# Expert stage of a cross-attention and mixture-of-experts kernel: groups kept in flight over more steps, with sixteen row buffers in place of eight

## Chip, cores and metric

The kernel runs on one core of one Trainium2 chip. The metric is the device time of one execution in microseconds (us), lower is better; several executions are timed and their median is given. Profiles are of one execution.

## What is computed

Input x is (32, 256, 256): 32 sequences of 256 tokens with 256 features; ctx has the same shape. Cut to what matters:

```python
x = x + xattn(layernorm(x), ctx, Wq1, Wk1, Wv1, Wq2, Wk2, Wv2, alpha, Wout, bout)
# and then the part that the change is in, over the 32*256 = 8192 tokens:
h = layernorm(x)
probs = softmax(h @ gate_w.T)                 # 16 experts
w, idx = top_k(probs, 4); w = w / sum(w)      # each token goes to 4 experts
g, u = h @ w1[e], h @ w3[e]                   # 256 -> 128, for expert e
out = sum over the 4 experts of w * ((silu(g) * u) @ w2[e])    # 128 -> 256
x = x + out
```

## The kernel before

**Stages.** The program has three stages, one after the other. The attention stage works through the 32 sequences in one loop; it also computes the router, sorts each normalised token into the region of each of its four experts in a DRAM table `x_rows` (a scatter by GpSimd, line 504), and counts. A short plan (lines 953 to 970) then makes a table of 144 groups: 8192*4/256 = 128 full groups of 256 rows and room for 16 more, since each expert's last group is padded. Each group belongs to one expert. The last stage (lines 461 to 469 and 1003 to 1019) reads four result rows for each token, weights them and adds.

**The expert stage** is what the change is about. All five engines run the same loop over groups, written by `stage_b` (line 355): the groups up to number `LOADS` are written out, then a hardware loop runs over passes of `LOADS` groups each, then the last ones are written out again. `LOADS` is 8, so TensorE's loop has 16 passes. `group(j, r)` holds what an engine does in step j (r = j mod `LOADS`), and the calls `if exists(j - 1)` say on which group each operation works. Matrix products are made from split operands: a number is kept as a rounded `hi` part and a rest `lo`, and three passes (hi*hi, hi*lo, lo*hi, `PASSES`) make one product.

In step j the engines do, in this order:

- SyncE (`load_group`, lines 442 to 455): reads the row number of group j from `table_row`, and starts the load of its 256 rows from `x_rows` into row buffer `xg[r]`. For j of 8 and above it first waits until TensorE has transposed group j - 8 (`xg_t`) and until the results of group j - 8 have been scattered (`y_sent`), since the scatter takes its row indices from the row buffer.
- TensorE (`group`, line 1280): transposes the rows of group j + 1 (`p_xt`, line 1289, 4 matmuls); reads the expert number of group j into a register (`expert_of`, line 1276) and makes gate and up of group j (`p_gu`, line 1300, 12 matmuls); transposes the gated values of group j - 1 (`p_at`, line 1310, 2 matmuls); makes the down projection of group j - 2 (`p_y`, line 1318, 6 matmuls). In the first two steps of a pass it also reads the expert of group j - 2 again, since registers don't outlive the pass (line 1281).
- ScalarE (line 691): tanh of group j - 1 into `gated` (696), `actT_hi` of group j - 2 (701), `y_out` of group j - 3 (706, waits for the scatter that used the same of four buffers), `xgT_hi` of group j + 1 (711).
- VectorE (line 978): the two products of the gating for group j - 1 (983, 986), `actT_lo` of j - 2 (992), `xgT_lo` of j + 1 (998).
- GpSimd (`return_group`, line 539): when `y_out` of group j is set, two indirect DMAs (line 544) scatter its 256 rows into `y_rows`.

Every PSUM result of this stage (`p_xt`, `p_gu`, `p_at`, `p_y`) has two buffers, taken in turn. The waits that a step rests on are the `wait` lines beside each operation, such as TensorE's before gate and up:

```python
pe.wait_ge(xgT_lo, j + 1)      # the split rows of group j
wait(pe, act_set, j - 1)       # p_gu's buffer, read by the gating of group j - 2
```

**Memory.** The weights' `lo` parts for the experts are made late from twelve 4 KB pieces a partition (`late_slots`, line 162) that are loaded a second time after the attention stage has released their space; the row buffers, `wgu_lo` and `wdn_lo` lie behind them.

Of the kernel before, what the change touches and what calls it, by code (L numbers as in the profile page):

```python
# [6 lines left out]
F32 = mybir.dt.float32  # L7
# [38 lines left out]
def xattn_moe_kernel(nc, x, ctx, Wq1, Wk1, Wv1, Wq2, Wk2, Wv2, alpha_attn, Wout, bout,  # L46
# [22 lines left out]
    MOST = TOKENS // GROUP  # L69
    DUMP = TOKENS * TOP_K  # L70
    PIECE = KT * INNER
    LOADS = 8
    TC = -(-GROUPS // P)
    assert S == 2 * P and D == 2 * P and INNER == 4 * P and I == P and B >= 4 and B % 4 == 0
    assert math.frexp(SCALE)[0] == 0.5
# [8 lines left out]
    with ExitStack() as stack:  # L84
        def sb(name, shape, dt=F32, stack=stack):
            return stack.enter_context(nc.sbuf_tensor(name, shape, dt))
# [72 lines left out]
            slotf = small("slotf", [P, ST, TOP_K])  # L159
            slot_i = small("slot_i", [P, ST, TOP_K], I32)  # L160
        with ExitStack() as later:
            late_slots = [sb(f"late_slot{i}", [P, PIECE], stack=later)[:, :] for i in range(E // 2 + E // 4)]
            wgu_lo = sb("wgu_lo", [P, E, KT, 2, I], F32R, later)
            wdn_lo = sb("wdn_lo", [P, E, D], F32R, later)
            wgu = [wgu_hi, wgu_lo]
            wdn = [wdn_hi, wdn_lo]
# [6 lines left out]
            y_out = [sb(f"y_out{i}", [P, 2, D], stack=later) for i in range(4)]  # L173

            plan = lambda name, shape, dt=F32: sb(name, shape, dt, later)
# [189 lines left out]
        def exists(j):  # L365

            return not isinstance(j, int) or 0 <= j < GROUPS
# [16 lines left out]
        def _(sp):  # L384
# [72 lines left out]

# [94 lines left out]
        def _(act):  # L552
# [136 lines left out]
            pad_experts(act, range(1, E, 2))  # L689

            def group(j, r):
                if exists(j - 1):
                    i = (r + 1) % 2
                    act.wait_ge(gu_done, j)
                    wait(act, act_t, j - 2)
                    act.activation(gated[i][:, :, :], p_gu[:, i, :, 0:I], ACT.Tanh, scale=0.5).then_inc(tanh_done, 1)
                if exists(j - 2):
                    i = r % 2
                    act.wait_ge(act_t, j - 1)
                    wait(act, down_done, j - 3)  # L700
                    act.copy(flat(actT[i][0][:, :, :]), p_at[:, i, 0:2 * P]).then_inc(actT_hi, 1)
                if exists(j - 3):
                    i, o = (r + 1) % 2, (r + 1) % 4
                    act.wait_ge(down_done, j - 2)
                    wait(act, y_sent[o], 8 * (j - 3 - o))
                    act.copy(flat(y_out[o][:, :, :]), flat(p_y[:, i, :, :])).then_inc(y_set, 1)
                if exists(j + 1):
                    i = (r + 1) % 2
                    act.wait_ge(xg_t, j + 2)
                    wait(act, gu_done, j)  # L710
                    act.copy(flat(xgT[i][0][:, :, :, :]), flat(p_xt[:, i, :, :, :])).then_inc(xgT_hi, 1)  # L711

            stage_b(act, group, before=1, after=3)


            for r in range(4):
# [12 lines left out]
        def _(dve):  # L729
# [246 lines left out]
                dve.tensor_tensor(lo, slot, hi.bitcast(F32), ALU.subtract).then_inc(late_lo, 1)  # L976

            def group(j, r):
                if exists(j - 1):
                    i = (r + 1) % 2  # L980
                    dve.wait_ge(tanh_done, j)

                    dve.scalar_tensor_tensor(gated[i][:, :, :], gated[i][:, :, :], 1.0, p_gu[:, i, :, 0:I],
                                             ALU.add, ALU.mult).then_inc(gate_step, 1)
                    dve.wait_ge(gate_step, j)
                    dve.tensor_tensor(gated[i][:, :, :], p_gu[:, i, :, I:2 * I], gated[i][:, :, :],  # L986
                                      ALU.mult).then_inc(act_set, 1)
                if exists(j - 2):
                    i = r % 2
                    dve.wait_ge(actT_hi, j - 1)  # L990
                    wait(dve, down_done, j - 3)
                    dve.tensor_tensor(flat(actT[i][1][:, :, :]), p_at[:, i, 0:2 * P],
                                      flat(actT[i][0][:, :, :]).bitcast(F32), ALU.subtract).then_inc(actT_lo, 1)
                if exists(j + 1):
                    i = (r + 1) % 2
                    dve.wait_ge(xgT_hi, j + 2)
                    wait(dve, gu_done, j)
                    dve.tensor_tensor(flat(xgT[i][1][:, :, :, :]), flat(p_xt[:, i, :, :, :]),  # L998
                                      flat(xgT[i][0][:, :, :, :]).bitcast(F32), ALU.subtract).then_inc(xgT_lo, 1)
            stage_b(dve, group, before=1, after=2)  # L1000


            def total(b, r, loads):
# [19 lines left out]
        def _(pe):  # L1023
# [254 lines left out]
            experts = {}  # L1278

            def group(j, r):  # L1280
                if exists(j - 2) and r < 2:
                    experts[(r - 2) % LOADS] = expert_of(j - 2)
                if exists(j + 1):
                    i = (r + 1) % 2
                    pe.wait_ge(xg_in[(r + 1) % LOADS], xg_loads(j + 1, r + 1))
                    wait(pe, xgT_lo, j)
                    for n in range(2):
                        for k in range(KT):
                            mm = pe.transpose(p_xt[:, i, n, k, :], xg[(r + 1) % LOADS][:, n, k * P:(k + 1) * P], ident[:, :])  # L1289
                    mm.then_inc(xg_t, 1)  # L1290
                if exists(j):
                    i = r % 2
# [12 lines left out]
                if exists(j - 1):  # L1305
                    i = (r + 1) % 2
# [5 lines left out]
                if exists(j - 2):  # L1312
                    i = r % 2
                    pe.wait_ge(actT_lo, j - 1)
                    wait(pe, y_set, j - 3)
                    for n in range(2):
                        for m, (h, a) in enumerate(PASSES):
                            mm = pe.matmul(p_y[:, i, n, :], actT[i][h][:, n, :],  # L1318
                                           wdn[a][:, bass.ds(experts[(r - 2) % LOADS], 1), :].rearrange("p e d -> p (e d)"),
                                           start=(m == 0), stop=(m == 2))  # L1320
# [32 lines left out]
```

## Time and profile before

| | |
|---|---|
| median of 3 executions | 2157.95 us (2154.18 to 2159.37) |
| profiled execution | 2155.32 us, of which its span is 2153.5 us |
| attention stage and plan | 0 to about 1576 us of the span |
| expert stage, first row transpose to end of last scatter's issue | 1579.5 to 2006.8 us |
| last stage | 2008 to 2153.5 us |
| TensorE busy over the span | 1907.1 us (89%) |
| VectorE, ScalarE, GpSimd busy | 1417.3, 1261.0, 1211.3 us |

Busy time is that of an engine's own work; reading a register, a branch or a wait doesn't count. The profile names TensorE's two halves PE (matmuls) and PEld (weight loads, which overlap them); DVE is VectorE, ACT ScalarE, POOL GpSimd, SP SyncE. A name with a q behind it (PEldq, POOLq, SPq) is the engine's sequencer: register reads, branches, DMA issues. In the slices of the page TensorE is nine tenths busy or more in almost all of the attention stage and of the expert stage, and falls off between the two and in the last stage.

### The profile page before, as it was taken

To read this page: it belongs to the slowest core of one execution; us is meant where nothing else is said; L and a number is where in the kernel's file an instruction comes from. 1 tells how busy PE (TensorE), PEld (TensorE's weight loads), DVE (VectorE), ACT (ScalarE), POOL (GpSimd) and SP (SyncE) were. 2 spreads that over 40 slices of the span, in tenths; PEclk is the share of its full clock that TensorE was granted. 3 is DMA by queue.
4 is the path that set the end of the run, shared out by engine and by line. 5 is a ranking of instruction groups with operands and counts; after the bars stand their busy time and mean duration, and the time that the engine had idled before them with its cause. 6 is when DMAs were issued, how large, how long until landed. Compare 5 with 4: busy or idle time off the path is not lost.

```text
span 2153.5 us, 53309 instructions
## 1 busy us (share of the span) xinstructions
PE 1907.1 (89%) x15778; PEld 1642.3 (76%) x15779; DVE 1417.3 (66%) x3205; ACT 1261.0 (59%) x3605; POOL 1211.3 (56%) x1683
## 2 busy tenths in 40 slices
PE   5999999999999999999999999999369999999100
PEld 4788888888888878888888888878269999999100
DVE  4567666667666666766666766666536666666577
ACT  4766666676666666666666666667136556555100
POOL 2466666566666566666566666556426666666200
PEclk9999999999999999999999999999679999999655
DMA  5610111101111110111101111110766666666798
GB/s 149 153 36 35 42 49 47 34 34 34 39 49 49 34 34 34 39 45 48 39 34 34 38 45 49 39 34 26 189 158 184 180 182 179 184 184 179 276 371 317
DMA packets 158596, 210.54 MB, mean 98 GB/s; under 512 B 24273, under 2 KB 131425, under 8 KB 158562
## 3 DMA queue, kind: packets, MB, share of 16 engines
q1 hardware_dynamic: 119394, 127.75, 20.7%
q0 software_dynamic: 26112, 71.86, 9.2%
q10 hardware_dynamic: 13056, 10.50, 1.7%
q8 instruction: 18, 0.29, 0.1%
q14 instruction: 16, 0.13, 0.0%
HBM read 113.02 MB, written 97.03 MB: 98 GB/s over the span
## 4 chain that ended last, share of the span: by engine, by line
PE 82%; DMA 7%; issue 3%; DVE 3%; SPq 3%; POOL 2%; ACT 1%; DVEq 0%; POOLq 0%; ACTq 0%
PE p_s L1047 12%; PE p_av L1145 12%; PE p_pt L1129 12%; PE p_s L1111 10%; PE p_gu L1300 9%; PE p_x L1180 5%; PE p_y L1318 4%; PE p_s L1057 4%; DMA z<-mid_rows 3%; PE p_xt L1289 3%; DMA out_dram<-z 2%; PE p_x L1047 2%; PE p_pt L1047 2%; PE p_av L1057 2%; PE p_pt L1057 2%
## 5 line engine op out<-in xcount | busy, mean ns | idle before, releaser
L512 POOL TENSOR_TENSOR probs<-probs,inv 128x256 f32<-128x256 f32 x1024 | 596.0, 614 | 434.0 <-DVE inv L844 433.3
L603 ACT ACTIVATE probs<-p_s,nmx 128x256 f32<-128x256 f32 x1024 | 475.3, 488 | 67.5 <-DVE nmx L837 62.7
L837 DVE TENSOR_REDUCE nmx<-p_s 128x4 f32<-128x1024 f32 x256 | 313.1, 1223 | 140.3 <-PE p_s L1111 136.7
L544 POOL DMA_INDIRECT y_rows<-y_out,xg x288 | 276.3, 959 | 177.8 <-issue 107.9
L504 POOL DMA_INDIRECT x_rows<-routed,slot_i x256 | 252.5, 986 | 170.0 <-DVE target L829 95.8
L1129 PEld LDWEIGHTS p_pt<-ident,probs 128*128 128x128 f32 x2048 | 222.2, 141 | 87.5 <-issue 62.4
L1129 PE MATMUL p_pt<-ident,probs 128*128 128x128 f32 x2048 | 280.0, 280 | 7.5 <-issue 4.9
L1145 PE MATMUL p_av<-probsT,val 128*64 128x256 f32 x2048 | 280.0, 394 | 6.5 <-DVE probsT L741 5.8
L741 DVE COPY probsT<-p_pt 128x512 f32<-128x512 f32 x256 | 176.1, 688 | 109.8 <-PE p_pt L1129 107.1
L1047 PE MATMUL p_s<-rowsT_hi,wp_hi 128*128 128x256 f32 x768 | 231.6, 302 | 8.3 <-DVE wp_lo L857 8.3
L591 ACT COPY probsT<-p_pt 128x512 f32<-128x512 f32 x256 | 152.5, 596 | 137.4 <-PE p_pt L1129 117.3
L603 ACT ACTIVATION_READ_ACCUMULATOR probs<-p_s,nmx 128x1 f32 x1024 | 223.4, 218 | 0.0
L1047 PE MATMUL p_s<-rowsT_hi,wp_lo 128*128 128x256 f32 x768 | 218.3, 284 | 0.0
L1047 PE MATMUL p_s<-rowsT_lo,wp_hi 128*128 128x256 f32 x768 | 218.2, 284 | 0.0
L1145 PEld LDWEIGHTS p_av<-probsT,val 128*64 128x64 f32 x2048 | 130.6, 137 | 76.1 <-issue 5.2
L1300 PE MATMUL p_gu<-wgu_hi,xgT_hi 128*128 x576 | 175.1, 304 | 6.1 <-DVE gated L986 4.3
L1111 PE MATMUL p_s<-kT_hi,qT_hi 64*128 64x256 f32 x1024 | 167.2, 323 | 2.4 <-DVE qT_lo L860 2.4
L1300 PE MATMUL p_gu<-wgu_hi,xgT_lo 128*128 x576 | 163.0, 283 | 0.0
L1300 PE MATMUL p_gu<-wgu_lo,xgT_hi 128*128 x576 | 161.9, 281 | 0.0
L998 DVE TENSOR_TENSOR xgT_lo<-p_xt,xgT_hi 128x512 fp32r<-128x512 f32 x144 | 99.6, 692 | 85.0 <-ACT xgT_hi L711 85.0
L1047 PEld LDWEIGHTS p_s<-rowsT_hi,wp_hi 128*128 128x128 f32 x768 | 147.7, 192 | 8.9 <-issue 8.7
L1047 PEld LDWEIGHTS p_s<-rowsT_lo,wp_hi 128*128 128x128 f32 x768 | 148.3, 193 | 0.0
(183 smaller groups left out, 4712.5 us busy)
## 6 DMA issues: line engine op xcount, KB each, us to landing
xg<-x_rows SPq DMA_DIRECT2D x144, 257.0 KB
y_in<-y_rows SPq DMA_DIRECT2D x32, 1024.0 KB, 6.7
rows<-in_ctx_dram SPq DMA_DIRECT2D x32, 256.0 KB, 2.7
x_in<-in_x_dram SPq DMA_DIRECT2D x32, 256.0 KB, 2.7
mid_rows<-x_mid SPq DMA_DIRECT2D x32, 256.0 KB, 2.2
z<-mid_rows SPq DMA_DIRECT2D x32, 256.0 KB, 7.4
out_dram<-z ACTq DMA_DIRECT2D x32, 256.0 KB, 5.7
y_rows<-y_out,xg POOLq DMA_INDIRECT x288
```

The lines of the kernel that those rows point to most:

```text
L504: pool.indirect_dma_start(x_rows, bass.IndirectOffsetOnAxis(ap=slot_i[:, t, k:k + 1], axis=0), routed[:, t, k, :], None).then_inc(rows_sen ...
L512: pool.tensor_tensor(pr[:, h, t, :], pr[:, h, t, :], rc[:, g:g + 1].to_broadcast([P, S]), ALU.mult).then_inc(normed_p, 1)
L544: pool.indirect_dma_start(y_rows, bass.IndirectOffsetOnAxis(ap=xg[r][:, i, D:D + 1].bitcast(I32), axis=0), y_out[r % 4][:, i, :], None).th ...
L603: act.activation(probs[u % 2][:, h, t, :], p_s[:, 2 * (u % 2) + h, t * S:(t + 1) * S], ACT.Exp, bias=nmx[u % 2][:, g:g + 1], accum_out=sum ...
L741: dve.tensor_copy(flat(probsT[:, 1, :, :]), p_pt[:, 1, :]).then_inc(pt_out_b, 1)
L837: dve.tensor_reduce(nmx[i][:, :], p_s[:, 2 * i:2 * i + 2, :].rearrange("p h (t k) -> p (h t) k", t=ST), AX.X, ALU.max, negate=True).then_i ...
L1047: mm = pe.matmul(proj_bank(n)[:, j * S:(j + 1) * S], wp[a][:, w, k, c:c + P], rowsT[w // 3][r][:, k, :], start=(i == 0), stop=(i == 5))
L1057: mm = pe.matmul(proj_bank(n), rowsT[w // 3][r][:, k, t * P:(t + 1) * P], wp[a][:, w, k, :], start=(i == 0), stop=(i == 5))
L1111: mm = pe.matmul(p_s[:, 2 * d + h, t * S:(t + 1) * S], qT[d][q][r:r + HEAD_DIM, p, t * P:(t + 1) * P], kT[d][k][r:r + HEAD_DIM, p, :], sta ...
L1129: mm = pe.transpose(p_pt[:, h, k * S + t * P:k * S + (t + 1) * P], probs[u % 2][:, h, t, k * P:(k + 1) * P], ident[:, :])
L1145: mm = pe.matmul(p_av[r:r + HEAD_DIM, 0:S], val[d][:, k, c:c + HEAD_DIM], probsT[:, h, k, :], start=(d == 0 and k == 0), stop=(d == 1 and ...
L1300: mm = pe.matmul(p_gu[:, i, n, :], xgT[i][h][:, n, k, :], wgu[a][:, bass.ds(experts[r], 1), k, :, :].rearrange("p e g i -> p (e g i)"), st ...
```

## The change

What it does, engine by engine:

- `LOADS` is 16: sixteen row buffers, and a hardware loop over passes of sixteen groups (7 passes), with more steps written out before and behind it.
- TensorE's step j now works on: rows of j + 2, gate and up of j, gated values of j - 2, down projection of j - 4. It reads the expert of j - 4 again in the first four steps of a pass.
- ScalarE's step: `xgT_hi` of j + 1 first, tanh of j - 1, `actT_hi` of j - 3, `y_out` of j - 5. VectorE's: `xgT_lo` of j + 1 first, the gating of j - 1, `actT_lo` of j - 3.
- GpSimd's step is as it was, in passes of sixteen. SyncE waits for group j - 16 before it loads group j.
- Memory: the eight new row buffers and the small tiles take the place of the weight pieces, so loads from the ninth on wait until the `lo` weights are made; `wgu_lo`, `wdn_lo` and the first eight row buffers stay where they were.

```diff
-    LOADS = 8
+    LOADS = 16
...
-            late_slots = [sb(f"late_slot{i}", [P, PIECE], stack=later)[:, :] for i in range(E // 2 + E // 4)]
...
-            xg = [sb(f"xg{i}", [P, 2, ROW], stack=later) for i in range(LOADS)]
+            with ExitStack() as loading:
+                late_slots = [sb(f"late_slot{i}", [P, PIECE], stack=loading)[:, :] for i in range(E // 2 + E // 4)]
+
+            xg_more = [sb(f"xg{i}", [P, 2, ROW], stack=later) for i in range(LOADS // 2, LOADS)]
...
             for r in range(LOADS):
+                if r == LOADS // 2:
+                    sp.wait_ge(late_lo, LATE)
                 load_group(r, r)
...
-                    sp.wait_ge(y_sent[r % 4], 32 * (2 * q + r // 4 - 1))
+                    sp.wait_ge(y_sent[r % 4], 32 * (LOADS // 4 * (q - 1) + r // 4 + 1))
...
# ScalarE, group(j, r)
+                if exists(j + 1):
+                    i = (r + 1) % 2
+                    act.wait_ge(xg_t, j + 2)
+                    wait(act, gu_done, j)
+                    act.copy(flat(xgT[i][0][:, :, :, :]), flat(p_xt[:, i, :, :, :])).then_inc(xgT_hi, 1)
                 if exists(j - 1):
...
-                if exists(j - 2):
-                    i = r % 2
-                    act.wait_ge(act_t, j - 1)
-                    wait(act, down_done, j - 3)
+                if exists(j - 3):
+                    i = (r + 1) % 2
+                    act.wait_ge(act_t, j - 2)
+                    wait(act, down_done, j - 4)
                     act.copy(flat(actT[i][0][:, :, :]), p_at[:, i, 0:2 * P]).then_inc(actT_hi, 1)
-                if exists(j - 3):
-                    i, o = (r + 1) % 2, (r + 1) % 4
-                    act.wait_ge(down_done, j - 2)
-                    wait(act, y_sent[o], 8 * (j - 3 - o))
+                if exists(j - 5):
+                    i, o = (r + 1) % 2, (r - 5) % 4
+                    act.wait_ge(down_done, j - 4)
+                    wait(act, y_sent[o], 8 * (j - 5 - o))
                     act.copy(flat(y_out[o][:, :, :]), flat(p_y[:, i, :, :])).then_inc(y_set, 1)
...
# TensorE, group(j, r)
-                if exists(j - 2) and r < 2:
-                    experts[(r - 2) % LOADS] = expert_of(j - 2)
-                if exists(j + 1):
-                    i = (r + 1) % 2
-                    pe.wait_ge(xg_in[(r + 1) % LOADS], xg_loads(j + 1, r + 1))
-                    wait(pe, xgT_lo, j)
+                i = r % 2
+                if exists(j - 4) and r < 4:
+                    experts[(r - 4) % LOADS] = expert_of(j - 4)
+                if exists(j + 2):
+                    pe.wait_ge(xg_in[(r + 2) % LOADS], xg_loads(j + 2, r + 2))
+                    wait(pe, xgT_lo, j + 1)
...
-                if exists(j - 1):
-                    i = (r + 1) % 2
-                    pe.wait_ge(act_set, j)
-                    wait(pe, actT_lo, j - 2)
+                if exists(j - 2):
+                    pe.wait_ge(act_set, j - 1)
+                    wait(pe, actT_lo, j - 3)
...
-                if exists(j - 2):
-                    i = r % 2
-                    pe.wait_ge(actT_lo, j - 1)
-                    wait(pe, y_set, j - 3)
+                if exists(j - 4):
+                    pe.wait_ge(actT_lo, j - 3)
+                    wait(pe, y_set, j - 5)
...
-            stage_b(pe, group, before=1, after=2)
+            stage_b(pe, group, before=2, after=4)
```

VectorE's step is reordered as ScalarE's is. The number of matmuls, copies, loads and scatters is the same.

## Rows read from the trace of the kernel before

**Rows 1.** Page, busy time by engine: us (share of the span) and instructions.

```profile
PE 1907.1 (89%) x15778; PEld 1642.3 (76%) x15779; DVE 1417.3 (66%) x3205; ACT 1261.0 (59%) x3605; POOL 1211.3 (56%) x1683
```

**Rows 2.** Busy time in one stretch of the expert stage (clock, DMA share, GB/s last).

```profile
1800.00:1900.00 100.00, 98.99 (x838) 97.35 (x837) 64.91 (x140) 59.90 (x141) 66.65 (x71) 1.00 0.62 180
```

**Rows 3.** Chain that ended last, one ordinary step: start us, us, what.

```profile
1795.88 0.71 PE p_y L1318 x6
1796.60 0.44 PE p_xt L1289 x4
1797.04 1.42 PE p_gu L1300 x12
1798.46 0.22 PE p_at L1310 x2
```

**Rows 4.** The same chain at the first two gate and up products.

```profile
1582.05 2.92 PE p_gu L1300 x12
...
1585.82 2.12 PE p_gu L1300 x12
```

**Rows 5.** Timeline, PE alone: first step of a pass (j = 72) and the next.

```profile
1790.30 0.60 PE L1289 MATMUL p_xt<-ident,xg 128*128 128x128 f32 x4
...
1791.17 0.38 PE L1300 MATMUL p_gu<-wgu_hi,xgT_hi 128*128 x1 [0.27 <-DVE gated L986]
...
1793.61 0.60 PE L1289 MATMUL p_xt<-ident,xg 128*128 128x128 f32 x4
...
1793.99 0.38 PE L1300 MATMUL p_gu<-wgu_hi,xgT_hi 128*128 x1
```

**Rows 6.** Waits from 1600 to 1995: total us, times, longest.

```profile
PEld p_gu L1300 <- issue: 11.9, 27, 0.8
...
PEld p_xt L1289 <- DMA xg<-x_rows: 0.7, 1, 0.7
```

**Rows 7.** TensorE's sequencer: min/median/max ns, first and last start; whole stage, then 1788 to 1791.

```profile
L359 PEldq COMPARE_BRANCH  x16: 76/208/231, 1626.2 to 1973.9; - x16
...
L359 PEldq ALU_OP  x1: 32/32/32, 1788.7 to 1788.7; - x1
...
L1276 PEldq SEQ_ASSERT  x2: 18/18/18, 1789.8 to 1790.8; - x2
```

**Rows 8.** Attention stage: sequencer at line 1102, and the matmuls still ahead of it.

```profile
L1102 PEldq ALU_OP  x1: 36/36/36, 933.8 to 933.8; - x1
...
933.93 0.28 PE L1047 MATMUL p_s<-rowsT_hi,wp_lo 128*128 128x256 f32 x1
...
937.02 0.39 PE L1057 MATMUL p_s<-wp_hi,rowsT_lo 128*128 128x512 f32 x1
```

**Rows 9.** Groups of instructions, 1600 to 1900: busy us, mean ns, idle before.

```profile
L711 ACT CAST xgT_hi<-p_xt 128x512 fp32r<-128x512 f32 x104 | 61.6, 593 | 0.4 <-PE p_xt L1289 0.4
L696 ACT ACTIVATE gated<-p_gu 128x256 f32<-128x256 f32 x104 | 40.0, 385 | 89.5 <-PE p_gu L1300 87.1 <-issue 2.4
L998 DVE TENSOR_TENSOR xgT_lo<-p_xt,xgT_hi 128x512 fp32r<-128x512 f32 x104 | 72.0, 692 | 45.1 <-ACT xgT_hi L711 45.1
L983 DVE SCALAR_TENSOR_TENSOR gated<-gated,p_gu 128x256 f32<-128x256 f32 x104 | 43.8, 421 | 57.6 <-ACT gated L696 57.6
```

**Rows 10.** The end of the stage: timeline of PE, then the chain that ended last.

```profile
1996.81 0.38 PE L1310 MATMUL p_at<-ident,gated 128*128 128x128 f32 x2
...
2004.55 0.96 POOL y_rows L544
...
2005.81 2.39 DMA y_rows<-y_out,xg
```

**Rows 11.** One attention pass by stretches; instruction fetches: 180 to 1470 us, then the page's.

```profile
900.00:946.21 46.21, 46.21 (x387) 38.36 (x386) 31.71 (x73) 31.07 (x94) 28.97 (x44) 1.00 0.12 40
...
q14 instruction: 1, 0.01, 0.0%
...
q8 instruction: 18, 0.29, 0.1%
```

More of the change, by code:

```diff
@@ L161, in xattn_moe_kernel @@
         with ExitStack() as later:
-            late_slots = [sb(f"late_slot{i}", [P, PIECE], stack=later)[:, :] for i in range(E // 2 + E // 4)]
[L163 to L166, printed above, removed]
-            xg = [sb(f"xg{i}", [P, 2, ROW], stack=later) for i in range(LOADS)]
+            with ExitStack() as loading:
+                late_slots = [sb(f"late_slot{i}", [P, PIECE], stack=loading)[:, :] for i in range(E // 2 + E // 4)]
+            xg_more = [sb(f"xg{i}", [P, 2, ROW], stack=later) for i in range(LOADS // 2, LOADS)]
             xgT = [[sb(f"xgT_hi{i}", [P, 2, KT, P], F32R, later), sb(f"xgT_lo{i}", [P, 2, KT, P], F32R, later)]
@@ L173, in xattn_moe_kernel @@
             y_out = [sb(f"y_out{i}", [P, 2, D], stack=later) for i in range(4)]
+            spare = sb("spare", [P, PIECE * len(late_slots) - LOADS * ROW - 2 * (4 * KT * P + 2 * I + 4 * P) - 8 * D],
+                       stack=later)
+            wgu_lo = sb("wgu_lo", [P, E, KT, 2, I], F32R, later)
+            wdn_lo = sb("wdn_lo", [P, E, D], F32R, later)
+            wgu = [wgu_hi, wgu_lo]
+            wdn = [wdn_hi, wdn_lo]
+            xg = [sb(f"xg{i}", [P, 2, ROW], stack=later) for i in range(LOADS // 2)] + xg_more
             plan = lambda name, shape, dt=F32: sb(name, shape, dt, later)
@@ L696, in group @@
                     act.activation(gated[i][:, :, :], p_gu[:, i, :, 0:I], ACT.Tanh, scale=0.5).then_inc(tanh_done, 1)
-                if exists(j - 2):
-                    i = r % 2
-                    act.wait_ge(act_t, j - 1)
-                    wait(act, down_done, j - 3)
+                if exists(j - 3):
+                    i = (r + 1) % 2
+                    act.wait_ge(act_t, j - 2)
+                    wait(act, down_done, j - 4)
                     act.copy(flat(actT[i][0][:, :, :]), p_at[:, i, 0:2 * P]).then_inc(actT_hi, 1)
-                if exists(j - 3):
-                    i, o = (r + 1) % 2, (r + 1) % 4
-                    act.wait_ge(down_done, j - 2)
-                    wait(act, y_sent[o], 8 * (j - 3 - o))
+                if exists(j - 5):
+                    i, o = (r + 1) % 2, (r - 5) % 4
+                    act.wait_ge(down_done, j - 4)
+                    wait(act, y_sent[o], 8 * (j - 5 - o))
                     act.copy(flat(y_out[o][:, :, :]), flat(p_y[:, i, :, :])).then_inc(y_set, 1)
-                if exists(j + 1):
-                    i = (r + 1) % 2
[L709 to L713, printed above, removed]
+            stage_b(act, group, before=1, after=5)
             for r in range(4):
@@ L978, in group @@
             def group(j, r):
+                i = (r + 1) % 2
+                if exists(j + 1):
+                    dve.wait_ge(xgT_hi, j + 2)
+                    dve.tensor_tensor(flat(xgT[i][1][:, :, :, :]), flat(p_xt[:, i, :, :, :]),
+                                      flat(xgT[i][0][:, :, :, :]).bitcast(F32), ALU.subtract).then_inc(xgT_lo, 1)
                 if exists(j - 1):
-                    i = (r + 1) % 2
                     dve.wait_ge(tanh_done, j)
@@ L987, in group @@
                                       ALU.mult).then_inc(act_set, 1)
-                if exists(j - 2):
-                    i = r % 2
-                    dve.wait_ge(actT_hi, j - 1)
-                    wait(dve, down_done, j - 3)
+                if exists(j - 3):
+                    dve.wait_ge(actT_hi, j - 2)
                     dve.tensor_tensor(flat(actT[i][1][:, :, :]), p_at[:, i, 0:2 * P],
                                       flat(actT[i][0][:, :, :]).bitcast(F32), ALU.subtract).then_inc(actT_lo, 1)
[L994 to L1000, printed above, removed]
+            stage_b(dve, group, before=1, after=3)
             def total(b, r, loads):
@@ L1280, in group @@
             def group(j, r):
-                if exists(j - 2) and r < 2:
-                    experts[(r - 2) % LOADS] = expert_of(j - 2)
-                if exists(j + 1):
-                    i = (r + 1) % 2
-                    pe.wait_ge(xg_in[(r + 1) % LOADS], xg_loads(j + 1, r + 1))
-                    wait(pe, xgT_lo, j)
+                i = r % 2
[4 more added lines that the diff above has]
+                    wait(pe, xgT_lo, j + 1)
                     for n in range(2):
                         for k in range(KT):
-                            mm = pe.transpose(p_xt[:, i, n, k, :], xg[(r + 1) % LOADS][:, n, k * P:(k + 1) * P], ident[:, :])
+                            mm = pe.transpose(p_xt[:, i, n, k, :], xg[(r + 2) % LOADS][:, n, k * P:(k + 1) * P], ident[:, :])
                     mm.then_inc(xg_t, 1)
                 if exists(j):
-                    i = r % 2
                     experts[r] = expert_of(j)
@@ L1318, in group @@
                             mm = pe.matmul(p_y[:, i, n, :], actT[i][h][:, n, :],
-                                           wdn[a][:, bass.ds(experts[(r - 2) % LOADS], 1), :].rearrange("p e d -> p (e d)"),
+                                           wdn[a][:, bass.ds(experts[(r - 4) % LOADS], 1), :].rearrange("p e d -> p (e d)"),
                                            start=(m == 0), stop=(m == 2))
```

3 lines of the change are left out of this document (removed).

## The prediction

> **What bounds the kernel now.** I read the page first: TensorE is busy 89% of the span and no other engine more than 66% [rows 1]. The change touches only the expert stage, so the next view is busy time by stretches: in an undisturbed 100 us there TensorE is busy 98.99 us at full granted clock, VectorE 64.91, ScalarE 59.90, GpSimd 66.65 (its issue gaps not counted), the DMA engines 62% [rows 2]. The chain that ended last shows what one step costs: down projection 0.71, row transposes 0.44, gate and up 1.42, gated transposes 0.22, all TensorE, back to back: 2.79 us a group [rows 3]. None of that work is removed. What the change can win is therefore only what TensorE loses beside it.
>
> That loss: the first gate and up starts at 1582.05 [rows 4], the last ends at 1996.81, where the transpose of group 142 follows it [rows 10]: 414.8 us. Between them lie 142 row transposes, 144 gate and up, 142 gated transposes, 141 down projections: 62.5 + 204.5 + 31.2 + 100.1 = 398.3 us. The first two products came after a stretch in which TensorE did next to nothing, and took 2.92 and 2.12 instead of 1.42, the first about twice as long as at full clock, so at 1.2 GHz: 2.2 more, and the transposes between them took 0.85 instead of 0.44 (1582.05 + 2.92 to 1585.82) [rows 4]: 2.6 in all. **13.9 us are stalls.** The view of waits finds most: 27 gaps before a gate and up weight load, 11.9 us, laid to "issue", and one late row load, 0.7 us [rows 6].
>
> **What the gaps are.** "Issue" means that no semaphore explains them, so I looked at the first step of a pass. At j = 72 gate and up starts 0.87 us after the transposes, a step later 0.38: 0.49 lost [rows 5]. The waits view names VectorE's gated product for some of these, but that is group j - 1, for which gate and up of j doesn't wait. The sequencer tells it: it reaches the branch at 1788.7 (the branch alone takes 0.21), reads the expert of j - 2 again, done at 1789.8, then that of j, done at 1790.8 [rows 7], and gate and up starts at 1791.17. From branch to product it needs 2.47 us. There are 17 such borders (loop entry, 15 returns, exit), so about 10 us are borders at 0.5 to 0.65, about 2 us ten small gaps in other steps, the rest the late load and what is too small to be listed.
>
> **The change, part by part.**
> (a) Fewer borders. Passes of sixteen have 8 borders (entry, 6 returns, exit), not 17. At an unchanged 0.57 that alone is 9*0.57 = 5.1 us.
> (b) More lead. Now the sequencer must stop in every step for values only one step old (gated of j - 1, the row split of j + 1, the row load of j + 1). After it, the newest values that TensorE waits for in step j follow from gate and up of j - 2: ScalarE's `xgT_hi` 0.59, then VectorE's `xgT_lo` 0.69 and two products of 0.42 each [rows 9], ready some 2.35 us after that product's end. Gate and up of j begins 0.22 + 0.71 + 0.44 + 1.42 + 0.22 + 0.71 + 0.44 = 4.16 us after it [rows 3]. So waits allow a lead of 1.8 us there, and more at the branch. How far can the sequencer be ahead at all? In the attention stage it handled line 1102 at 933.8, when the matmul of 933.93, four transposes and twelve products, the last at 937.02, had not begun [rows 8]: 17 matmuls with their loads. Counting 17 back from gate and up of j: the transposes of the next rows are issued behind the branch, so the queue holds 6 of the down projection, 2 gated transposes, 9 of gate and up: 0.71 + 0.22 + 9*0.118 = 1.99, and with the 0.44 of row transposes 2.43 us of cover for the 2.47 needed. So the branch step should stall by about 0.04.
> What the Trainium skill says: "TensorE: Matmul & The Clock Gate" (the table at its head) gives TensorE's queue 64 entries, 32 matmuls with their loads. The row shows 17. By the page borders would be free even with slow register reads, and the sum would end near 10.5 us instead of 8.5.
> (c) Two more steps of a pass (r = 2, 3) read an expert twice. Today's r = 1 does so and takes 1793.99 - 1791.17 = 2.82 instead of 2.79 [rows 5]. I take up to 0.07 each for r = 1 to 3, with 0.04 for the branch 0.25 a border, 2.0 in all. Bounds: nothing, or today's 0.57 (4.6 in all). 0.25 is near the lower end, because the cover worked out above nearly reaches.
> (d) The small gaps and the late load: the row load of j starts when the scatter of j - 16, not j - 8, is done, and eight steps more are 22 us; no load can be late by the 0.7 of rows 6. Small gaps need a lead below 0.1 us, which (b) removes. I leave 0.8; bounds 0 and 2.
> (e) Start. Gate and up of group 0 now stands behind the row transposes of group 2, at the lower clock about 1.0 us (between the 0.85 above and some 1.1): start 1583.05. It is moved, not added. The row load of group 2 must have landed by then; it could be late by 0 to 1 us, and I take 0, since today nothing waits for it.
> (f) Order on ScalarE and VectorE: the sum of a step is under 2 us on each [rows 2, 9], with 0.8 spare; ScalarE's wait for `y_sent` comes last in its step and delays nothing before the next `xgT_hi`, which has 1.8 us.
> (g) The eight loads that wait for the `lo` weights: TensorE itself waits for these before its first transpose. Nothing.
> (h) **The drain, which costs.** After the last gate and up five down projections remain, not three, and GpSimd needs 2*1.26 = 2.52 us for each group (2004.55 to 2005.81) [rows 10]. Today the last scatter starts at 2005.81, 9.0 us after the last gate and up. After it, `y_out` of group 138 is set about 1.0 us before that end (2.79 earlier plus tanh, `actT_hi` and its own copy, a little over 0.39 + 0.4 + 0.59); six groups follow, the last scatter starting 11*1.26 = 13.9 later: 12.9, say 13.0. That is 4.0 us lost, less 0.22 + 2*0.71 = 1.6 of TensorE work that moves behind the last gate and up.
>
> **Sum.** 1583.05 + (141*0.44 + 144*1.42 + 141*0.22 + 139*0.71 = 396.2) + 2.2 low clock + 2.8 stalls = 1984.2, the end of the last gate and up. Plus 13.0: 1997.2 against 2005.81: **8.6 us earlier**. The landing (2.39) and the last stage stay. Profiled execution: 2155.3 - 8.6 = 2146.7. The median of the runs is 2.6 above the profiled one, which I take for spread: 2157.95 - 8.6 = 2149.4, rounded to 2149.5.
>
> What a measurement of this kernel can tell from no change is about 0.3%, 6.5 us.
>
> **Rivals.**
> A, forecast (0.60): borders and small gaps nearly go, the drain costs 2.4 net. 2143.5 to 2152.
> B (0.32): the lead isn't there. Borders stay at 0.57 (4.6) and small gaps at 2.0, because slower register reads beside DMA traffic, or queue entries used by other instructions eat the 0.04 balance of (b). For: the balance is within the accuracy of its terms. Against: the lead before it is larger in every other step. Stalls 6.6 instead of 2.8: gain 4.8, 2153.
> C, the other side (0.08): the longer loop no longer stays in TensorE's instruction memory, and each of the 7 passes fetches code again. Price: the page's queue q8 moved 18 packets in 0.1% of 16 engines' span [rows 11], 0.001*16*2153.5/18 = 1.9 us each. One exposed fetch a pass costs 13 us and gives 2163; two give 2176; it decides (over 0.3% slower) from (8.6 + 6.5)/7 = 2.2 us a pass. Against it: an attention pass has 387 + 386 matmuls and weight loads, and in all passes from 180 to 1470 us the only instruction packet is one of another queue [rows 11]. Sixteen groups have 16*24*2 = 768 of them, though with more register instructions between them. That they fit is likely, not certain.
> The Trainium skill's "Runtime: NRT & Kernel Launch" (Instruction fetch mechanics) speaks against this change: a taken branch whose target lies outside a window of two fetched pages waits for a fetch. By that rule the attention passes would have fetched each time; the rows show they didn't.
> D is inside A and B: that sixteen row buffers do nothing, since loads were late only once.
>
> **Chances.** Faster by over 0.3% (below 2151.5): nearly all of A, little of B: 0.60. Same 0.33. Slower 0.07. The range runs from no stalls at all (a gain of 11.4: 2146.5, less the 2.6 between runs) to B with a slow run: 2143.5 to 2156.5; C lies outside.
>
> **What would show it.** Steps of 2.79 us right through; the gaps "PEld p_gu from issue" down from 27 to ten or fewer; no wait for row loads; last gate and up near 1984; last scatter near 1997, about 13 us behind it. Wrong if the first step of each pass still loses 0.5 us (B), if instruction packets appear on q8 between 1640 and 1980 (C), or if ScalarE waits for `y_sent` and TensorE for `xgT_lo`.

## The result, and the profile after

The changed kernel takes **2147.78 us** (median of 5 executions, 2144.26 to 2151.82). The kernel before, measured again with it, takes 2158.52 (2154.18 to 2159.37). The ratio is 0.9953, with a 95% interval of 0.9935 to 0.997: faster by 0.5%. Predicted were 2149.5 and a range of 2143.5 to 2156.5. The profiled execution took 2151.82 us, the slowest of the five; its span is 2150.1.

The page first, then an undisturbed 100 us of the expert stage (answers to [rows 1] and [rows 2]; the last row is the changed kernel's too, with the columns of [rows 2]).

```profile
PE 1895.6 (88%) x15778; PEld 1638.6 (76%) x15779; DVE 1403.2 (65%) x3205; ACT 1260.9 (59%) x3605; POOL 1210.3 (56%) x1683
...
q8 instruction: 24, 0.39, 0.1%
```

```profile
1800.00:1900.00 100.00, 100.00 (x863) 100.00 (x862) 63.72 (x144) 62.46 (x144) 68.86 (x72) 1.00 0.64 190
```

The same matmuls are there, and in this stretch none of the time is lost: TensorE is busy 100.00 of 100 us, against 98.99. Its total on the page is 11.5 us smaller at the same 15778 matmuls, so part of what it lost before had been counted as busy.

The chain that ended last, at the start of the stage, at an ordinary step and at the end (start us, us, what; answers to [rows 4], [rows 3] and [rows 10]):

```profile
1582.07 1.12 PE p_xt L1292 x4
1583.18 2.10 PE p_gu L1302 x12
1585.28 0.44 PE p_xt L1292 x4
1585.72 1.42 PE p_gu L1302 x12
...
1800.21 0.71 PE p_y L1318 x6
1800.92 0.44 PE p_xt L1292 x4
1801.36 1.42 PE p_gu L1302 x12
1802.78 0.22 PE p_at L1311 x2
...
1978.93 1.41 PE p_gu L1302 x12
1980.35 0.23 PE p_at L1311 x2
...
1994.76 2.40 DMA y_rows<-y_out,xg
```

The pieces of a step are as long as before, 2.79 in all. Gate and up of group 0 starts at 1583.18, the last one ends at 1980.35 (before: 1996.81), the last scatter starts at 1994.76 (before: 2005.81). **The stage ends 11.05 us earlier**: the last gate and up ends 16.46 earlier, and 5.4 of that are given back behind it.

The waits of TensorE from 1600 to 1985 (total us, times, longest; answers to [rows 6]). There is no line for `p_gu` from "issue", where 27 gaps stood, and none for a late row load:

```profile
PEld p_y L1318 <- issue: 0.6, 2, 0.3
PEld p_at L1311 <- DVE gated L997: 0.4, 1, 0.4
PE p_at L1311 <- DVE actT_lo L1001: 0.2, 1, 0.2
```

And one pass border (j = 64). The sequencer reaches the branch at 1756.9 (start of the first row, in us; the columns before it are min/median/max ns); its two register reads are done at 1757.9 and 1759.0 (first and last start of the second row). The timeline of PE shows gate and up of that step 0.42 us behind its transposes, where the step before it has 0.35; in [rows 5] it was 0.87.

```profile
L364 PEldq COMPARE_BRANCH  x1: 208/208/208, 1756.9 to 1756.9; - x1
...
L1279 PEldq SEQ_ASSERT  x2: 18/18/18, 1757.9 to 1759.0; - x2
```

```profile
1756.13 0.60 PE L1292 MATMUL p_xt<-ident,xg 128*128 128x128 f32 x4
1756.48 0.36 PE L1302 MATMUL p_gu<-wgu_hi,xgT_hi 128*128 x1
...
1757.04 0.28 PE L1302 MATMUL p_gu<-wgu_lo,xgT_hi 128*128 x1
...
1758.91 0.60 PE L1292 MATMUL p_xt<-ident,xg 128*128 128x128 f32 x4
1759.33 0.38 PE L1302 MATMUL p_gu<-wgu_hi,xgT_hi 128*128 x1
```

From 1757.04 to the last product of the down projection lie 8 matmuls of gate and up, 2 transposes and 6 of the down projection: 16, and one more begins at 1756.92, with the branch: 17 that TensorE still had to begin when its sequencer arrived there. The first read is done before they run out (the last begins at 1758.79), the second while TensorE transposes the next rows. It comes just late enough to cost 0.07 us: this step takes 2.86 us. The first steps of the other six passes and of the part behind the loop take 2.78 to 2.80 and lose nothing; before the change such steps took 3.03 to 3.65.

**The whole time moved less than the stage in this one execution** (3.5 us, 2155.32 to 2151.82). The rest is in the last stage, which the change doesn't touch: from its start to the end of the span before 145.1 us, after 152.8. It is bound by its transfers, and their rate differs; a stretch of it in either kernel, after and then before:

```profile
2060.00:2100.00 40.00, 0.00 (x0) 0.00 (x0) 27.09 (x67) 0.00 (x0) 0.00 (x0) 0.50 0.91 324
```

```profile
2070.00:2110.00 40.00, 0.00 (x0) 0.00 (x0) 31.02 (x78) 0.00 (x0) 0.00 (x0) 0.50 1.02 366
```

That this is spread and not an effect of the change is what a second profile of the changed kernel says (147.0 us there), and those of the experiments: 144.8 to 152.4, with no order by kernel (the shortest and one of the longest are kernels of the new depth). So I compare kernels by medians, and traces by the expert stage alone, from the first gate and up to the start of the last scatter: 423.8 us before, 411.7 after.

### The profile page after: what moved, and what is told of

Read it like the earlier page. It is cut to its first block, busy times and chain, and to the rows that moved or that the text cites. A ratio compares the mean times of both kernels' runs of the same rounds, so it can differ in the third digit from the quotient of the medians.

```text
span 2150.1 us, 52636 instructions
## 1 busy us (share of the span) xinstructions
PE 1895.6 (88%) x15778; PEld 1638.6 (76%) x15779; DVE 1403.2 (65%) x3205; ACT 1260.9 (59%) x3605; POOL 1210.3 (56%) x1683
## 4 chain that ended last, share of the span: by engine, by line
PE 84%; DMA 7%; SPq 2%; DVE 2%; issue 2%; POOL 1%; ACT 1%; DVEq 0%; POOLq 0%; ACTq 0%
PE p_s L1050 12%; PE p_av L1148 12%; PE p_pt L1132 12%; PE p_s L1114 10%; PE p_gu L1302 10%; PE p_x L1183 5%; PE p_y L1318 5%; PE p_s L1060 4%; DMA z<-mid_rows 3%; PE p_xt L1292 3%; DMA out_dram<-z 2%; PE p_x L1050 2%; PE p_pt L1050 2%; PE p_av L1060 2%; PE p_pt L1060 2%
## 5 line engine op out<-in xcount | busy, mean ns | idle before, releaser
L703 ACT CAST xgT_hi<-p_xt 128x512 fp32r<-128x512 f32 x144 | 84.4, 586 | 188.5 <-PE p_gu L1302 142.1
```

## Experiments

Two theories. **Lead**: TensorE stalled because its sequencer, held in each step for values one step old, came to the border with too little queued to cover the branch and two reads; the new depth gives it the lead. **Buffers and passes**: fewer borders and later-reused row buffers do it, and the depth only lengthens the drain. All diffs are against the changed kernel where nothing else is said.

**1. Sixteen buffers with the old depth.** The order of before on all three engines, the memory layout of the change; here against the kernel before:

```diff
-    LOADS = 8
+    LOADS = 16
...
+                if r == LOADS // 2:
+                    sp.wait_ge(late_lo, LATE)
...
-                    sp.wait_ge(y_sent[r % 4], 32 * (2 * q + r // 4 - 1))
+                    sp.wait_ge(y_sent[r % 4], 32 * (LOADS // 4 * (q - 1) + r // 4 + 1))
```

> Sixteen row buffers and passes of sixteen, but each engine's step works on the same groups as before the change. Theory L (the stalls are the sequencer's: 17 borders of passes at about 0.5 us, each free only if the sequencer has a lead of more than 2.4 us): 8 borders remain, still at 0.4 to 0.6 us each because the waits for values one step old keep the lead short; stalls between the first and the last gate and up fall from 13.9 to 5 or 6 us, the drain stays at 9 us, so the last scatter starts about 8 us earlier than before, against 11 in the changed kernel. Rival R (row loads that come late take the lead away, depth does nothing): stalls fall to under 1 us here too, and without the longer drain this kernel is faster than the changed one by 3 to 4 us.

Measured: 2148.53 (2145.19 to 2150.89), ratio 0.9961 (0.9948 to 0.9973): as fast as the whole change. The last scatter starts at 1994.82 (changed: 1994.76), 11.0 us earlier than before and not 8; 1.2 of that are a shorter stretch at the low clock. But the way there is another: gate and up of the last group starts at 1984.41 (changed: 1978.77). TensorE's waits from 1600 to 1988:

```profile
PEld p_gu L1307 <- issue: 4.5, 12, 0.6
PE p_gu L1307 <- DVE gated L993: 2.0, 7, 0.4
```

The old depth stalls on at its borders (steps of 3.28 to 3.45), and has a drain of 9 us for 14.4. From group 5 to group 141 it takes 4.7 us more than the changed kernel, and behind the last gate and up 5.4 less. The two cancel. So the new depth does remove stalls, as the first theory has it, and yet it isn't where the gain comes from.

**2. The new depth with eight buffers.**

```diff
-    LOADS = 16
+    LOADS = 8
...
-            for j in range(-before, LOADS):
+            for j in range(-before, 2 * LOADS):
...
-            with eng.Fori(1, GROUPS // LOADS - 1) as q:
+            with eng.Fori(2, GROUPS // LOADS - 1) as q:
```

> The new depth with eight row buffers. A row buffer comes free when its group is scattered. By the rows: y_out of group j-8 is set 1.2 us into step j-3, two scatters take 2.5, the landing 1.4 more, SyncE's read and issue 0.9, the load 2.9: 8.9 us after the start of step j-3, and step j-2 can't begin earlier. Theory: every step takes about 9 us instead of 2.79, so the expert stage lasts some 1300 us and the run some 3030 us. Rival (row buffers hardly matter, since before the change only one load was late): below 2200 us.

Measured: 2750.24 us (one execution), some 600 slower. The chain that ended last shows one turn of it:

```profile
1898.00 2.43 DMA y_rows<-y_out,xg
...
1901.26 3.39 DMA xg<-x_rows
...
1904.77 1.11 PE p_xt L1292 x4
1905.88 2.83 PE p_gu L1302 x12
...
1909.13 1.29 PE p_y L1318 x6
...
1913.35 2.40 DMA y_rows<-y_out,xg
```

A row buffer is free only when its group's results have been scattered, and the next row load, product, down projection and scatter follow one another with nothing beside them: 15.35 us from scatter to scatter (1898.00 to 1913.35), for two steps. TensorE is idle enough to fall to the lower clock in between (gate and up takes 2.83, granted clock 0.865 over the span, 0.947 in the changed kernel). Rows two ahead and results five steps back need about nine groups between load and scatter, and eight buffers don't hold them. My expectation took each step to pay the wait; two steps share one. What follows: **the depth can't be had without the buffers**, and the sixteen buffers are not idle memory.

**3. One more register read at each border.** The value isn't used; the work is the same.

```diff
                 i = r % 2
+                if r == 0 and not isinstance(j, int):
+                    expert_of(j - 3)
```

> The changed kernel with one more register read by TensorE's sequencer (about 0.75 us with its register work) in the first step of each of the 7 passes. If the queue ahead of the sequencer holds about 17 matmuls, the cover at a border (2.34 us) is used up by the 2.35 us it needs today, and the read shows in full: 0.7 us at each of 7 borders, 5 us in all, and gate and up of that step begins that much later. If the queue held 32 matmuls, as a page says, the sequencer would stand 0.8 us further ahead and the read would cost nothing.

Measured: 2153.58 us (one execution); the first steps of the seven passes take 3.26, 3.53, 3.54, 3.45, 3.70, 3.55 and 3.65 us (end of gate and up to end of gate and up) where they were 2.78 to 2.86: 5.1 in all, 0.73 for each read; the stage takes 417.4 us for 411.7. At j = 64, in the chain that ended last:

```profile
1758.57 1.43 PE p_gu L1304 x12
...
1761.75 1.69 PE p_gu L1304 x12
1763.44 0.22 PE p_at L1313 x2
```

3.44 us from 1760.00 to 1763.44. Had the queue held 32 matmuls, the sequencer would by the expectation's own estimate have stood 0.8 us further ahead, and the read would have cost nothing. It costs its full length, so at the border of the changed kernel the balance is just even, as part (b) of the prediction worked it out from 17 matmuls in the queue [rows 8]. Again 17 have not begun when the sequencer is at the branch, at each of the six returns and at the exit.

**4. The down projection three groups behind, not four.** `y_out` of j - 4 then follows; the drain is one group shorter.

```diff
-                if exists(j - 4):
-                    pe.wait_ge(actT_lo, j - 3)
-                    wait(pe, y_set, j - 5)
+                if exists(j - 3):
+                    i = (r + 1) % 2
+                    pe.wait_ge(actT_lo, j - 2)
+                    wait(pe, y_set, j - 4)
...
-            stage_b(pe, group, before=2, after=4)
+            stage_b(pe, group, before=2, after=3)
```

> The changed kernel with down projections three groups behind instead of four. Gain of the shorter drain: one group less for GpSimd, 2.5 us, less 0.7 of TensorE work: 1.8 us. Theory L: actT_lo of group j-3 is ready 2.7 us after gate and up of j-1, its down projection begins 3.0 us after it, so the sequencer stops there in every step and reaches the border only about 1.0 us ahead: 8 borders at about 0.8 us and 16 steps with a second read at up to 0.4 us, 6 to 12 us lost, so 4 to 10 us slower than the changed kernel. Rival (the fourth step of lag is not needed): 1.8 us faster than the changed kernel, every step 2.79 us.

Measured: 2165.97 (2157.79 to 2171.97), ratio 1.0043 (1.0028 to 1.0057): **slower than before**, and a larger loss than I had expected. Waits of TensorE from 1600 to 1995, then the chain that ended last at the same border:

```profile
PEld p_gu L1302 <- issue: 10.6, 18, 1.0
PEld p_xt L1292 <- issue: 4.3, 8, 0.7
...
PE p_gu L1302 <- DVE xgT_lo L989: 2.1, 6, 0.5
```

```profile
1763.74 1.43 PE p_gu L1302 x12
...
1767.49 1.69 PE p_gu L1302 x12
...
1770.55 1.67 PE p_gu L1302 x12
...
1773.86 1.69 PE p_gu L1302 x12
...
1776.91 1.42 PE p_gu L1302 x12
```

The ends of these products lie 4.01, 3.04, 3.32 and 2.79 apart: 2.0 us too many for one border, spread over three steps. The reason can be counted. ScalarE and VectorE now put the row split first, so the values for the down projection come behind it: after gate and up of j - 1 has ended, `xgT_hi` 0.59, `xgT_lo` 0.69, two products of 0.42 [rows 9] and `actT_lo` 0.34 make 2.5 us. TensorE is there after 0.22 + 0.71 + 0.44 + 1.42 + 0.22 = 3.0. A lead of 0.5 us is four or five matmuls; the trace has 5 not yet begun when the sequencer is at the branch, against 12 before and 17 in the changed kernel. The new order on ScalarE and VectorE therefore needs the fourth group; three behind is worse than the old order with two.

**5. Passes of sixteen with eight buffers**, against before:

```diff
     LOADS = 8
+    PASS = 16
...
-            with eng.Fori(1, GROUPS // LOADS - 1) as q:
-                for r in range(LOADS):
-                    body(LOADS * q + r, r)
+            with eng.Fori(1, GROUPS // PASS - 1) as q:
+                for r in range(PASS):
+                    in_pass[0] = r
+                    body(PASS * q + r, r % LOADS)
...
-                if exists(j - 2) and r < 2:
+                if exists(j - 2) and in_pass[0] < 2:
```

> The kernel before with loop passes of sixteen groups, but eight row buffers and the old depth: 8 borders instead of 17 and nothing else. Theory: a border costs 0.5 to 0.6 us, so stalls fall by 9 of them, 5 us, from 13.9 to 9, and the last scatter starts near 2001. What is left over the run with sixteen buffers at old depth (5.4 us of stalls, last scatter at 1994.8) is then the row buffers' own share, 3 to 4 us. Rival (borders do it all, the buffers nothing): last scatter at 1995, as with sixteen buffers.

Measured: 2152.87 (2143.83 to 2160.46), ratio 0.9974 (0.9958 to 0.999); stage 418.7 us for 423.8, last scatter 2000.24 for 2005.81. Nine borders fewer are worth 5.1 to 5.6 us, the 5.1 of part (a). The first steps of the passes lose 9.3 us in all before, 3.8 here and 4.0 in experiment 1. And from here to experiment 1, eight more row buffers at the same depth and the same passes: 418.7 to 413.1, 5.6 us more (1994.82 for 2000.24: 5.4), where I had expected 3 to 4. These are differences between single profiles; by whole times, on two chips, the ratios of 5 and 1 (0.9974 and 0.9961) don't tell the two apart. Waits of experiment 5 that experiment 1 has shorter or not at all:

```profile
PEld p_gu L1306 <- issue: 7.8, 19, 0.8
...
PEld p_xt L1295 <- DMA xg<-x_rows: 0.9, 1, 0.9
...
PE p_xt L1295 <- DMA xg<-x_rows: 0.7, 1, 0.7
```

The last two rows are one late row load (both at 1658.83), seen by the two halves of TensorE; its step loses 1.6. Seven gaps laid to "issue" fewer in experiment 1 are the rest. The sequencer waits at the row load too, and a load that comes just in time costs no visible wait but takes the lead away, which shows as "issue" at the next product. The semaphore events of the loads in the traces bear this out. I take the steps of groups 10 to 141 that are not the first or second of a pass. Before the change 11 of these 100 take over 2.84 us, 4.1 us too many in all, and their rows had landed only 0.04 to 0.63 us before the transposes began; in the other 89 it was 0.61 us or more. Experiment 5 has 11 of 116, 4.6 us, landed 0.05 to 0.74 us before, the other 105 at least 0.61. In experiment 1 the rows land more than 16 us before, and none of 116 is over 2.84. No run delayed a load alone.

**6. Experiment 1 with TensorE's 144 steps written out**, no loop and no second reads:

```diff
-                if exists(j - 2) and r < 2:
-                    experts[(r - 2) % LOADS] = expert_of(j - 2)
...
-            stage_b(pe, group, before=1, after=2)
+            for j in range(-1, GROUPS + 2):
+                group(j, j % LOADS)
```

> Sixteen row buffers at the old depth, TensorE's 144 steps written out one after the other: no border and no expert read twice. Theory: the 5.4 us of stalls that were left at the old depth are borders and second reads, all gone; every step 2.79 us; the drain stays at 9 us, so the last scatter starts near 1989.5, 5 us earlier than in the changed kernel and 16 earlier than before, and the run takes 5 us less than the changed kernel. Rival F (code that is never met twice has to be fetched all the time, a fetch for every 4 groups, and TensorE waits for some): gaps before any kind of matmul at regular distances of about 11 us, 0.5 to 2 us each, 15 us and more lost.

Measured: 2142.72 (2141.93 to 2146.67), ratio 0.9931 (0.9917 to 0.9946): **the fastest median, ahead of both kernels**. From the same set of executions the changed kernel gave

> The changed kernel once more, beside the two others on the same chip. Last gate and up ends near 1980.4, last scatter starts near 1994.8 as in its first profile; the length of the last stage (152.9 us there, 145.1 before) differs from run to run, because it hangs on DMA bandwidth alone: expected between 144 and 154, and not tied to the change.

2147.4 (2145.13 to 2151.53), ratio 0.9959 (0.9945 to 0.9974). By whole times the two intervals just touch; the stage is the clearer measure, 408.3 us for 411.9. The page, and TensorE's waits of experiment 6 from 1600 to 1990:

```profile
q8 instruction: 47, 0.77, 0.1%
```

```profile
PEld p_at L1315 <- DVE gated L993: 0.7, 1, 0.7
...
PEld p_y L1323 <- issue: 0.5, 2, 0.3
```

Every step takes 2.78 to 2.79. Instruction packets doubled, and no step shows a gap. At the old depth with sixteen buffers and no borders nothing stalls, and the drain is the short one:

```profile
1988.98 0.96 POOL y_rows L551
...
1990.24 2.40 DMA y_rows<-y_out,xg
```

**7. The changed kernel written out, beside experiment 6 again.** This measures the depth alone, with the borders gone from both.

```diff
-                if exists(j - 4) and r < 4:
-                    experts[(r - 4) % LOADS] = expert_of(j - 4)
...
-            stage_b(pe, group, before=2, after=4)
+            for j in range(-2, GROUPS + 4):
+                group(j, j % LOADS)
```

> The changed kernel with TensorE's steps written out, so without borders and second reads. Theory: the new depth has nothing left to hide (0.2 us of stalls in the changed kernel), so writing out brings nothing here: last gate and up ends near 1980, last scatter starts near 1994.5, and the run is 4 us slower than the written-out kernel at the old depth, which is the price of the longer drain. Rival (the written-out code gains in another way than by the borders, for instance by fewer sequencer instructions in every step): this one is as fast as the other or faster.

> The written-out kernel at the old depth once more, beside the one at the new depth on the same chip. Last scatter starts between 1989.5 and 1990.5, all steps 2.79 us; 3 to 5 us less than the new depth written out.

Measured, on a chip where the kernel before takes 2162.16: 2152.39 (2146.83 to 2157.26), ratio 0.9962 (0.9944 to 0.9979), and 2149.44 (2144.16 to 2153.48), ratio 0.9949 (0.9932 to 0.9965). The stages take 412.6 and 408.6 us: the depth costs 4.0 us once nothing stalls. By whole times the two intervals overlap. Experiment 6's kernel beats the kernel before in both sets (0.9931 and 0.9949); the changed kernel itself was not run on this chip.

The stage in one table (us; one profile each; how long the low clock lasts at its start differs between profiles, by up to 1.2 us of time for the same order of work):

| kernel | stage | last scatter starts |
|---|---|---|
| before | 423.8 | 2005.81 |
| passes of sixteen, eight buffers, old depth (5) | 418.7 | 2000.24 |
| sixteen buffers, old depth (1) | 413.1 | 1994.82 |
| changed | 411.7, again 411.9 | 1994.76, 1993.79 |
| sixteen buffers, old depth, written out (6) | 408.3, again 408.6 | 1990.24, 1995.55 |
| changed, written out (7) | 412.6 | 1999.13 |

The last scatters of (7) and of (6) again stand later because their stages began later, at 1586.5 and 1587.0, where the others began at 1581.6 to 1583.1.

## Why the prediction held, and where its terms were off

The forecast was faster, by 8.5 us; it came out 10.7 by the medians, 11.05 by the end of the stage. Term by term:

- **Bound and work.** Right: steps of 2.79, and the 396.2 us of work fit what lies between the first and the last gate and up.
- **(a) Nine borders fewer, 5.1.** Right: 5.1 to 5.6 (experiment 5).
- **(b) The queue of 17.** Right, by the extra read that costs 0.73 us in experiment 3. The branch step was to stall by 0.04; one of the eight does by 0.07 (j = 64), seven don't. The 2.47 needed are counted from the register operation before the branch, [rows 7]; from the branch itself, at 1788.8, it is 2.36, and the changed kernel has 2.35 from branch to product at most borders. That a count limits the lead, and not one of the waits, shows in places with other waits: 17 matmuls have not begun at the register read of 138 of the 144 steps in experiment 7's first kernel, and at line 1102 of the attention stage at 27 of the 29 times it is met. There they are 3.4 us of work, here 2.0 to 2.4. The rule of 64 entries given in the Trainium skill, "TensorE: Matmul & The Clock Gate", isn't borne out by the trace: with 32 matmuls the extra read should have been free.
- **(c) and (d) Stalls of 2.8.** Too high; 0.2 is left. The 0.25 a border was taken between two bounds, and the lower bound was the right one. The steps r = 1 to 3 with their extra reads lose next to nothing either, 0.1 in one of them (j = 34): a step with two reads and no branch has the lead for them.
- **(d) again, rival D.** "Sixteen row buffers do nothing, since loads were late only once" was wrong, the one misjudgement of mechanism. They are worth 5.4 to 5.6 us at the old depth (experiments 5 and 1), and without them the new depth is 600 us slower (experiment 2). I counted only the wait that the profile names, 0.7, and put the small gaps laid to "issue" down to a short lead that (b) would lengthen. They were row loads that had landed just before their transposes: eleven steps, 4.1 us, before the change (experiment 5).
- **(e) Start.** By the chain gate and up of group 0 began at 1583.18 (1583.05 foreseen), but its low clock cost 0.7 and not 2.2. The rows of two stretches, before and then after, say why: the granted clock (third number from the end) was back at full speed sooner, at 1584.3 and not at 1587.3.

```profile
1584.00:1586.00 2.00, 2.00 (x11) 2.00 (x11) 0.54 (x2) 0.52 (x2) 0.00 (x0) 0.50 0.74 213
```

```profile
1584.00:1586.00 2.00, 2.00 (x18) 2.00 (x17) 0.00 (x1) 0.62 (x2) 0.00 (x0) 0.93 0.83 242
```

  The change isn't needed for this: with the old start the clock was back at 1583.9 and 1584.1 in experiments 1 and 6, and with the new one only at 1585.7 in experiment 3, all with their first transposes between 1578.7 and 1579.5. So the 1.5 us between forecast and result are chance, as far as these profiles tell.
- **(h) The drain, 13.0.** It took 14.4 (1980.35 to 1994.76). The scatters of the changed kernel on the timeline:

```profile
1978.32 0.96 POOL L551 DMA_INDIRECT y_rows<-y_out,xg  x1 [0.56 <-issue]
...
1980.84 0.96 POOL L551 DMA_INDIRECT y_rows<-y_out,xg  x1 [0.30 <-issue]
...
1994.76 0.96 POOL L551 DMA_INDIRECT y_rows<-y_out,xg  x1 [0.30 <-issue]
```

  The first of group 138 starts at 1980.84, and eleven spacings of 1.26 follow, as foreseen. I had it start 1.0 before the last gate and up ended; it came 0.5 after. Two things were left out: in the last two steps there are no row transposes, so the products come 2.34 apart and not 2.79 (0.45), and GpSimd starts a scatter about 0.8 after `y_out` is done and was still busy with group 137 for another 0.2.
- **(f), (g).** Right: TensorE shows no wait for `xgT_lo` (the 0.2 and 0.4 above are for other tiles) and no late first load; ScalarE never waits for `y_sent` before the drain.

The sum of the misses: -1.5 for the clock, -2.6 for stalls, +1.4 for the drain, +0.1 at the start and +0.2 for what the sum rounds; 2.4 in all, 1997.2 foreseen, 1994.76 measured. That these are small in sum is in part luck: the stalls and the drain were off in opposite directions, and the 1.5 of the clock is not the change's.

**Rivals.** B (borders stay) fell in the changed kernel; it is what happens one read later (experiment 3) or one group shorter (experiment 4), so it was close. C (instruction fetches in each pass) fell, though its sign as I had put it, packets on q8 between 1640 and 1980, was met by 7 packets. q8 carries TensorE's code (writing out TensorE's steps alone took it from 24 packets to 47), and over the whole span there were 24 where there had been 18. But between 1670 and 1944, nearly all of the last six of the seven passes, there is none, and no step shows a gap: the packets come with the steps written out before and behind the loop and with its first pass. The Trainium skill's "Runtime: NRT & Kernel Launch" (Instruction fetch mechanics) recommends straight code over loops; experiment 6 agrees that straight code costs nothing (47 packets, no gap), but its reason, a fetch at each branch out of a window of two pages, is not seen in either kernel's loops. The same section of the Trainium skill gives TensorE room for 2048 instructions, and with that the traces agree: a pass of the changed kernel's loop has about 1010 records of TensorE, an attention pass about 830.

## What to carry to other kernels

Before an engine's pipeline is made deeper, ask whether its depth is short in ordinary steps or only at loop borders. Here, once the row loads came early enough, it was short only where the sequencer had register reads to do twice, behind a branch above all; writing the loop out cured that and longer passes made it rarer, while every group of depth is paid again in the drain at the pace of the slowest engine in it (2.5 us a group on GpSimd, 4.0 us in all for two groups in experiment 7). And where buffers are freed by the far end of the pipeline, depth and buffers go together: count the groups from load to release before choosing either.

## What the runs showed of the hardware

- TensorE's sequencer got 17 matmuls with their loads ahead of what TensorE began, at the branches, register reads and line 1102 counted here, and not more; they were 2.0 us of work in one place and 3.4 in another.
- A border with two register reads takes 2.2 to 2.7 us from branch to product where TensorE stalls at it, with a third read 3.0 to 3.25; the branch itself 0.208 in the median.
- At the old depth with eight buffers a row load that landed less than 0.6 us before TensorE's transposes cost its step 0.1 to 1.6 us, mostly shown as "issue" and not as a wait for a DMA.
- 144 steps of straight code ran without a gap, at 47 instruction packets for 24 with the loop; a loop of about 1010 records a pass ran from 1670 to 1935, six passes, without a packet.
- One kernel's last stage, bound by transfers, took 147.0 and 152.8 us in two profiles. An effect of a few us elsewhere is better read from its own stage than from whole times of single executions.
